# A two-layer audio tower: three normalizations moved from VectorE to ScalarE, a loop of four slots, fewer waits

## The reference, cut to what matters

```python
h = tok(x)                      # stride-2 convolution + mean of the pair, layernorm, gamma, beta -> (64, 188, 256)
h = h + attn0(layernorm(h))     # 16 heads of 16, softmax attention over the 64 sequences
h = h + ffn0(layernorm(h))      # gate, up (704) and down, inputs and weights rounded to blockwise fp4
h = h + attn1(layernorm(h))     # 16 heads of 64, causal linear attention over the 188 rows
h = h + ffn1(layernorm(h))      # layernorm again, dequantized fc1 (1024), silu, fc2, 0.5 * z

def _layernorm(x, axis=-1, eps=1e-05):
    m = jnp.mean(x, axis=axis, keepdims=True)
    ...
    return (x - m) / jnp.sqrt(v + eps)
```

## Time and profile before

| | us |
|---|---|
| median of 3 runs | 4795.0 (4787.19 to 4800.82) |
| the profiled execution | 4793.58 |
| its span on the core | 4791.8 |
| PE busy | 4454.1 (93%) |
| DVE busy | 3397.0 (71%) |
| ACT busy | 2495.3 (52%) |
| POOL busy | 1855.2 (39%) |

### The profile page before, as it was taken

One profiled execution on the slowest core, in us unless ns is written; L12 is line 12 of the kernel. 1 busy time (PEld: TensorE's weight loads), 2 busy tenths in 40 slices (PEclk: granted clock), 3 DMA queues, 4 the chain that ended last, 5 costly groups with the idle time before them and its releaser, 6 DMA issues.

```text
span 4791.8 us, 120275 instructions
## 1 busy us (share of the span) xinstructions
PE 4454.1 (93%) x43016; PEld 3973.3 (83%) x43016; DVE 3397.0 (71%) x7197; ACT 2495.3 (52%) x5314; POOL 1855.2 (39%) x2018
## 2 busy tenths in 40 slices
PE   3999999999999948999999999999999999999997
PEld 2888888888888847888888888888888888888886
DVE  5899999999999853666666666665666666666665
ACT  2555555555555524555554554554555555555553
POOL 1444444444444422343343343333334333334333
PEclk9999999999999979999999999999999999999998
DMA  2000000000000010000000000000000000000000
GB/s 82 19 23 23 23 23 23 23 23 23 23 23 23 22 41 8 5 15 8 8 11 11 8 8 15 8 8 15 8 8 11 11 8 8 14 8 8 15 5 11
DMA packets 64881, 78.93 MB, mean 16 GB/s; under 512 B 8759, under 2 KB 51127, under 8 KB 64439
## 3 DMA queue, kind: packets, MB, share of 16 engines
q1 hardware_dynamic: 64566, 74.07, 5.4%
HBM read 49.40 MB, written 24.64 MB: 15 GB/s over the span
## 4 chain that ended last, share of the span: by engine, by line
PE 45%; issue 9%; POOL 5%; DVE 2%; ACT 1%; POOLq 0%; DMA 0%; DVEq 0%; ACTq 0%; SPq 0%
PE bA L930 9%; PE bA L931 8%; PE bA L932 8%; PE bS L1216 3%; PE bO L1239 2%; PE bA L1303 2%; PE bB L930 2%; POOL sqs_lo L1636 2%; PE bB L1202 2%; PE bB L932 2%; PE bB L931 2%; PE bB L1203 2%; PE bA L1304 1%; PE bT L1256 1%; POOL yT_lo L1594 1%
## 5 line engine op out<-in xcount | busy, mean ns | idle before, releaser
L1636 POOL TENSOR_TENSOR sqs_lo<-sq,sqs_hi 128x768 fp32r<-128x768 f32 x256 | 471.4, 1842 | 811.7 <-ACT sqs_hi L1356 803.9
L1447 DVE TENSOR_TENSOR qk_lo<-bA,qk_hi 128x384 fp32r<-128x384 f32 x512 | 283.4, 553 | 626.4 <-ACT qk_hi L1356 626.2
L1375 ACT ACTIVATE phi<-bB 128x768 f32<-128x768 f32 x256 | 207.9, 812 | 681.2 <-PE bB L1203 681.2
L1594 POOL TENSOR_TENSOR yT_lo<-tanh_y,yT_hi 128x384 fp32r<-128x384 f32 x256 | 258.2, 1009 | 631.2 <-ACT yT_hi L1356 631.2
L1356 ACT ACTIVATE qk_hi<-bA 128x384 fp32r<-128x384 f32 x512 | 251.2, 491 | 229.6 <-PE bA L932 229.6
L1457 DVE TENSOR_TENSOR aT<-bS,mask 128x1024 f32<-128x1024 f32 x256 | 310.9, 1215 | 1.8 <-PE bS L1221 1.6
L930 PE MATMUL bA<-fc_lo,yT_hi 128*128 128x256 f32 x768 | 231.5, 301 | 60.9 <-POOL yT_lo L1594 34.2
L1365 ACT ACTIVATE sq<-bA 128x384 f32<-128x384 f32 x512 | 250.2, 489 | 61.7 <-DVE qk_lo L1447 61.6
L516 PE MATMUL bank<-down_sb,hqT 128*128 128x256 f32 x1128 | 278.5, 389 | 1.0 <-ACT hqT L598 1.0
L614 ACT ACTIVATE kblk<-gu,kb_masked,rowmask 128x128 f32<-128x128 f32 x752 | 270.7, 462 | 6.3 <-PE gu L540 6.3
L516 PEld LDWEIGHTS bank<-down_sb,hqT 128*128 128x128 f32 x1128 | 204.4, 190 | 52.6 <-issue 32.6
(11 more groups left out here) (243 smaller groups left out, 15025.4 us busy)
## 6 DMA issues: line engine op xcount, KB each, us to landing
xT<-in_x SPq DMA_DIRECT2D x94, 256.0 KB, 2.7
h_scratch<-h SPq DMA_DIRECT2D x188, 64.0 KB, 1.9
hx<-h_scratch SPq DMA_DIRECT2D x32, 256.0 KB, 2.7
out<-res SPq DMA_DIRECT2D x32, 256.0 KB, 2.1
hx<-h_scratch SPq DMA_DIRECT2D x64, 64.0 KB, 2.4
out<-res SPq DMA_DIRECT2D x64, 60.0 KB, 1.8
q<-in_fc_q SPq DMA_DIRECT2D x2, 1024.0 KB, 6.2
wq_sb<-in_wq SPq DMA_DIRECT2D x1, 1024.0 KB, 5.0
```

The source lines that it names most:

```text
L1447: dve.tensor_tensor(dst, src, hi.bitcast(fp32), ALU.subtract).then_inc(S[done], 1)
L1594: pool.tensor_tensor(yT[1][:, f % RING, :], tanh_y[f % 2][:], yT[0][:, f % RING, :].bitcast(fp32), ALU.subtract).then_inc(S["y_lo"], 1)
L1636: pool.tensor_tensor(sqs[1][:], sq[:], sqs[0][:].bitcast(fp32), ALU.subtract).then_inc(S["sq_lo"], 1)
```

## The change

Layer 0: `ln0_normalize` and `ln1_normalize` leave VectorE, and `xq_normalize` does too, as `ln2_normalize`. ScalarE now computes them as `Identity` activations with a row scale `rstd` and a row bias `nbias` = -mean x rstd, which POOL computes with two more one-column instructions in each `rsqrt`. VectorE's third `bn_aggr` moves ahead of its second gate step. Layer 1: the loop's body holds four slots instead of two (slots 3 to 26, six passes); `fc1` part 3 moves from step 4, place 1, to step 3, place 2, and `fc2` pair 0 the other way; waits that another wait implies are left out on TensorE.

```diff
@@ def normalize, ACT, layer 0 (the DVE functions of the same names are gone) @@
+                def normalize(dst, src, k, done):
+                    act.activation(dst, src, ACT.Identity, bias=nbias[:, k, :], scale=rstd[:, k, :]).then_inc(S[done], 1)
+
+                def ln0_normalize(t):
+                    wait(act, "rs0", t + 1, 4)
+                    wait(act, "gb_step", t, 3)
+                    wait(act, "ln1_ready", t)
+                    normalize(h0[:], y0[:], 0, "ln0")
...
+                def ln2_normalize(t, par):
+                    wait(act, "rs2", t - 1, 4)
+                    wait(act, "xq_step", t - 2, XQ)
+                    normalize(ln2[:], h1[par][:], 2, "ln2_ready")
@@ def slot, ACT, layer 0 @@
                     if exists(t, 2):
                         att_copy(t)
+                    if exists(t, 0):
+                        ln0_normalize(t)
                     if exists(t, 4):
                         hq_copy(t)
...
                     if exists(t, 3):
                         tanh(t - 3, 1)
+                    if exists(t, 0):
+                        ln1_normalize(t)
+                    if exists(t, 2):
+                        ln2_normalize(t, par)
+                    if exists(t, 3):
                         h1_copy(t, 1 - par)
@@ DVE, layer 0 @@
-                def normalize(dst, src, k):
-                    return dve.tensor_scalar(dst, src, moments[:, k, 0:1], rstd[:, k, :], ALU.subtract, ALU.mult)
...
                     if exists(t, 2):
                         row_statistics(h_st, 2, h1[par][:])
+                        row_moments(h_st, 2)
                     if exists(t, 3):
                         glu_gate(t - 3, 1)
                         glu_up(t - 3, 1)
-                    if exists(t, 0):
-                        ln1_normalize(t)
-                    if exists(t, 2):
-                        row_moments(h_st, 2)
-                    if exists(t, 3):
                         hq_scales(t - 3)
@@ def rsqrt, POOL, layer 0 @@
                     pool.tensor_tensor(rstd[:, k, :], moments[:, k, 1:2], eps[:, 0:1], ALU.add).then_inc(S[name], 1)
-                    pool.wait_ge(S[name], 2 * t + 1)
+                    pool.tensor_scalar(nbias[:, k, :], moments[:, k, 0:1], -1.0, None, ALU.mult).then_inc(S[name], 1)
+                    pool.wait_ge(S[name], 4 * t + 1)
                     pool.tensor_tensor(rstd[:, k, :], rstd[:, k, :], exponent[:, 0:1], ALU.pow).then_inc(S[name], 1)
+                    pool.wait_ge(S[name], 4 * t + 3)
+                    pool.tensor_tensor(nbias[:, k, :], nbias[:, k, :], rstd[:, k, :], ALU.mult).then_inc(S[name], 1)
@@ def slots, layer 1 @@
-            last = 3 + (SLOTS - 5) // 2 * 2
+            last = 3 + (SLOTS - 5) // UNROLL * UNROLL
...
-            with nc.Fori(3, last, 2, engines=(eng.engine,), hint_back_edge=True) as s:
-                slot(s, 1)
-                slot(s + 1, 0)
+            with nc.Fori(3, last, UNROLL, engines=(eng.engine,), hint_back_edge=True) as s:
+                for u in range(UNROLL):
+                    slot(s + u, (1 + u) % 2)
@@ def places, layer 1 @@
-            for f, (c, n) in enumerate(((2, 1), (2, 2), (3, 1), (4, 1), (4, 2), (5, 2), (6, 1), (7, 2))):
+            for f, (c, n) in enumerate(((2, 1), (2, 2), (3, 1), (3, 2), (4, 2), (5, 2), (6, 1), (7, 2))):
                 p[c][n] = ("fc1", s - 2, f)
-            p[3][2], p[5][1] = ("fc2", s - 2, 0, par), ("fc2", s - 2, 1, par)
+            p[4][1], p[5][1] = ("fc2", s - 2, 0, par), ("fc2", s - 2, 1, par)
@@ PE, layer 1: c1_qk; the same in c2_proj (qk_lo), c3_scores (phi_ready), c4_av (att1_step), @@
@@ c5_transpose (attT_hi), xn_transpose, h5_transpose, fc1 (hT_hi), fc2_pair (y_hi), wo_pair (attT_hi) @@
                     if c == 0:
-                        wait(pe, "xT_hi", s + 1, KC)
                         wait(pe, "xT_lo", s + 1, KC)
...
-                        read[i].extend((("qk_hi", 4 * g + (3 + i)), ("qk_lo", 2 * g + (1 + i))))
+                        read[i].append(("qk_hi", 4 * g + (3 + i)))
```

More of the change, by code:

```diff
@@ L54 @@
 RING = 4
+UNROLL = 4
 def wait_for(eng, sem, count, last, per=1):
@@ L677, in xq_copy, with ln1_normalize @@
                     copy(xqT[0][:], tp[:, 0:256].rearrange("p (c t) -> p c t", c=KC), "xqT_copied")
+                def normalize(dst, src, k, done):
[5 more added lines that the diff above has]
+                    normalize(h0[:], y0[:], 0, "ln0")
+                def ln1_normalize(t):
+                    wait(act, "rs1", t + 1, 4)
+                    wait(act, "ln1_transposed", t)
+                    normalize(ln1[:], h0[:], 1, "ln1_ready")
+                def ln2_normalize(t, par):
+                    wait(act, "rs2", t - 1, 4)
+                    wait(act, "xq_step", t - 2, XQ)
+                    normalize(ln2[:], h1[par][:], 2, "ln2_ready")
                 def slot(t, par):
@@ L733, in conv_read @@
                     wait(dve, "conv_done", t + 1)
+                    wait(dve, "ln0", t)
                     st = Steps(dve, S["y_step"], t, YS)
@@ L752, in score_shift @@
                     st.end()
[L754 to L757, removed]
                 def glu_gate(z, r):
@@ L786, in h1_add @@
                     return st
[L788 to L791, removed]
                 def h2_add(w, par):
@@ L797, in h2_add, with xq_scales @@
                     dve.tensor_tensor(h2[par][:], cv[:, 0:DM], h1b[par][:], ALU.add).then_inc(S["h2_ready"], 1)
-                def xq_normalize(y, par):
-                    wait(dve, "rs2", y + 1, 2)
+                def xq_scales(y):
+                    wait(dve, "xq_ready", y)
+                    wait(dve, "ln2_ready", y + 1)
                     st = Steps(dve, S["xq_step"], y, XQ)
-                    st.add(normalize(ln2[:], h1[par][:], 2))
+                    fp4_scales(dve, st, ln2[:], small_x, 128, DM)
                     return st
[L805 to L808, removed]
                 def xq_scaled(st):
@@ L1191, in c1_qk @@
                         last.then_inc(S["qk_done"], 1)
-                        read[i].extend((("qk_hi", 4 * g + (3 + i)), ("qk_lo", 2 * g + (1 + i))))
+                        read[i].append(("qk_hi", 4 * g + (3 + i)))
                 def c2_proj(g):
-                    wait_g(pe, "qk_lo", g + 1, 2)
                     wait_g(pe, "sq_lo", g + 1)
@@ L1206, in c3_scores @@
                 def c3_scores(g, b):
-                    wait_g(pe, "phi_ready", g + 1)
+                    if not has_chunk(g + 1):
+                        wait_g(pe, "phi_ready", g + 1)
                     wait_g(pe, "aT_ready", g)
@@ L1226, in c4_av @@
                     wait_g(pe, "aT_ready", g + 1)
-                    wait_g(pe, "att1_step", g, 3)
                     if c % 2 == 0:
@@ L1252, in c5_transpose @@
                     wait_g(pe, "att1_step", g + 1, 3)
-                    wait_g(pe, "attT_hi", g)
                     wait_g(pe, "attT_lo", g)
@@ L1286, in xn_transpose @@
                     for k in range(KC):
-                        read[k].extend((("xT_hi", s * 2 + (k + 1)), ("xT_lo", s * 2 + (k + 1))))
+                        read[k].append(("xT_lo", s * 2 + (k + 1)))
                 def h5_transpose(s):
@@ L1292, in h5_transpose @@
                     for k in range(KC):
-                        read[k].extend((("hT_hi", s * 2 + (k + 1)), ("hT_lo", s * 2 + (k + 1))))
+                        read[k].append(("hT_lo", s * 2 + (k + 1)))
                 def fc1(s, f):
                     if f == 0:
-                        wait(pe, "hT_hi", s + 1, KC)
                         wait(pe, "hT_lo", s + 1, KC)
@@ L1320, in fc2_pair @@
                 def fc2_pair(s, j, par):
-                    pe.wait_ge(S["y_hi"], s * FC + (2 * j + 2))
                     pe.wait_ge(S["y_lo"], s * FC + (2 * j + 2))
@@ L1325, in wo_pair @@
                 def wo_pair(s, j, par):
-                    pe.wait_ge(S["attT_hi"], s * CH + (2 * j + 2))
                     pe.wait_ge(S["attT_lo"], s * CH + (2 * j + 2))
```

10 lines of the change are left out of this document (4 added, 6 removed).

## The result

The changed kernel takes **4708.7 us** (median of 4 runs, 4704.83 to 4711.23) where the kernel before, run beside it, takes 4792.2 (4787.19 to 4800.82): a ratio of 0.9823, 95% interval 0.9806 to 0.984. The forecast was 4729 with a range of 4698 to 4770. The sign and the range held; the gain is 84 us where I forecast 66.

The account below looks back on a forecast made before the run. TensorE was taken to bound both layers, losing time in layer 1 at the loop end, `sq` waits and `fc2` stall. Terms -36 - 16 - 12 - 2 + 2 = -64 us gave 4729 us, range 4698 to 4770.

Parts of the forecast that it names:

- Loop end, 7 jumps x 5.1 = -36 us: Layer 1: a four-slot loop has seven jumps back fewer, each worth 5.1 us, saving 36 us.
- -2 us that I gave the swap for the clock: Layer 1: with the `fc2` stall shorter, some clock drops behind it may go, saving 2 us.
- Waits left out, -16 us: Layer 1: one needless wait less before V and `wo` products, 0.07 us each, eight a loop slot, saving 16 us.
- `fc1` 3 and `fc2` 0, -12 us (0.4 a slot): Layer 1: exchanging them leaves 1.4 of a 1.8 us stall, saving 0.4 us in each of 32 slots, 12 us.
- Case B: Layer 1: the `fc2` stall goes whole, another 44 us saved, total 4685 us; chance 6%.
- Layer 0, 0 a slot: Layer 0: moving three normalizations to ScalarE changes no slot, since TensorE sets the pace and ScalarE's new work fits.
- +2 for the first slots: Layer 0's first slots, where nothing overlaps: 0.5 us longer for each of four normalizations in the chain, costing 2 us.
- case C: Layer 0: VectorE sets the pace, so its 1.2 us relief saves 113 us over 94 slots, about 4616 us; chance 5%.
- A: Layer 1: jumps cost by body length, 10.2 instead of 5.1 us, giving back 26 us, total 4755 us; chance 10%.
- charge on VectorE: Layer 1 loop: by the skill's 512-instruction fetch window, VectorE's branch begins to pay in the longer pass; no firm size.
- D: Layer 0: ScalarE late if POOL's new instructions cost 0.55 us, +108 us, about 4837; chance 5% in full, 8% mild.

Follow-up runs that it names:

- e4_layer0: Kernel before with only layer 0's change, its three normalizations moved to ScalarE: 4793.6 us, ratio 0.9994.
- e6_head87: Kernel before, all waits kept, with the layer 1 loop's first TensorE instruction set at place 87 of its 256-instruction block: 4752.1 us, ratio 0.9921.
- e10_head167: Kernel before, all waits kept, with the layer 1 loop's first TensorE instruction set at place 167 of its 256-instruction block: 4749.1 us, ratio 0.9915.
- e12_after_two_head87: Changed kernel with two slots per jump instead of four and the loop's first TensorE instruction set at place 87 of its block: 4720.5 us, ratio 0.9853.
- e2_waits: Kernel before with only the implied waits left out on TensorE in layer 1, loop of two slots: 4728.5 us, ratio 0.986.
- e7_waits_head167: Kernel before with the implied waits left out and the loop's first TensorE instruction set at place 167 of its block: 4721.4 us, ratio 0.9859.
- e9_after_two: Changed kernel with two slots per jump instead of four, all else as changed: 4710.5 us, ratio 0.9833.
- e3_swap: Kernel before with only `fc1` part 3 and `fc2` pair 0 changing places: 4772.5 us, ratio 0.995.
- e1_unroll: Kernel before with only layer 1's loop changed, to four slots per pass: 4751.2 us, ratio 0.9905.
- e13_act_twice: Changed kernel with each of layer 0's three normalizations made twice by ScalarE, once into an unread tensor: 4731.6 us, ratio 0.9878.
- e11_after_head87: Changed kernel with its loop's first TensorE instruction set at place 87 of its block: 4705.0 us, ratio 0.982.

## Why the prediction was right, and where it was not

*Loop end, 7 jumps x 5.1 = -36 us.* **This step failed in its price.** The count, seven jumps fewer, is right. But I held the price fixed and changed only the number. The jumps cost 12 x 5.35 = 64.2 us before and 5 x 1.80 = 9.0 after: -55. The price before has three parts: the first stop, a median 2.2 us; the second stop, 0.9 to 1.6 behind two jumps of three, which I had not seen; and the clock, which in the loop was at 0.50 for 51 us before and for 3.4 after. If half of that time is lost, it is an estimated 26 / 12 = 2.1 us a jump; the three shares are rough, for e4_layer0 pays about the same for its jumps (63.3 us) with longer first stops and 37.5 us at the low clock. Three of its eleven stretches, 3.4 us each, stand not at the jump but 49 us behind it, at the `fc2` stall:

```profile
2267.30:2270.70 3.40, 3.40 (x16) 3.40 (x17) 1.59 (x4) 0.41 (x1) 0.00 (x0) 0.50 0.00 0
```

At this stall stand also all the low stretches of e6_head87 (five) and e10_head167 (three), whose jumps are cheap; the runs with `fc1` 3 and `fc2` 0 exchanged have none there. So the -2 us that I gave the swap for the clock was a real term, and more like -5 (three stretches of 3.4 us, half lost: an estimate).

In the changed kernel only the first stop is left:

```profile
2741.39 0.34 PE L1308 MATMUL bA<-hT_hi,fc_w 128*128 128x384 f32 x1
2743.27 0.43 PE L938 MATMUL bB<-qk_lo,omega_hi 128*128 128x384 f32 x1 [1.54 <-issue]
...
2745.10 0.34 PE L938 MATMUL bA<-xT_lo,wq_hi 128*128 128x384 f32 x1
```

And the number of jumps, which I credited, is not what the gain hangs on: with two slots to a pass the same kernel takes 4710.5 us, its twelve jumps 10.6 us. It hangs on where the loop's code lies, and the other parts of the change moved that; the number counts only where jumps are dear, as in e12_after_two_head87.

*Waits left out, -16 us.* Right as a term, wrong as an account of the edit. The mechanism is as forecast. The load behind `sq` in the loop, after, against the earlier trace rows:

```profile
3570.11 0.48 ACT L1367 ACTIVATE sq<-bA 128x384 f32<-128x384 f32 x1
3570.65 0.19 PEld L938 LDWEIGHTS bA<-wv_lo,xT_hi 128*128 128x128 f32 x1 [0.17 <-ACT sq L1367]
```

Over some 200 of these places in the loop the median from the end of `sq` to the load is 0.051 us, before 0.122: 0.071 saved, and 0.07 forecast. Eight in a slot are 0.57, and slots went from 89.39 to 88.78 in e2_waits. Alone the edit brought 68 us, because taking instructions out moved the loop: its jumps cost 13.7 us in all, and so do those of e10_head167, which has every wait and another place.

*`fc1` 3 and `fc2` 0, -12 us (0.4 a slot), and -2 for the clock.* The mechanism is right, the size a little off. The step after the change, against the earlier trace rows:

```profile
3586.00 0.65 ACT L1407 ACTIVATE pre<-bA,fc1b,fc1s 128x384 f32<-128x384 f32 x1
...
3586.70 0.44 PE L1307 MATMUL bA<-hT_lo,fc_w 128*128 128x384 f32 x1 [1.17 <-ACT pre L1407]
3586.75 0.62 DVE L1517 SCALAR_TENSOR_TENSOR pre<-bA,fc1s,pre 128x384 f32<-128x384 f32 x1 [0.75 <-ACT pre L1407]
...
3586.98 0.34 PE L1308 MATMUL bA<-hT_hi,fc_w 128*128 128x384 f32 x1
...
3587.42 0.19 PEld L1307 LDWEIGHTS bA<-hT_lo,fc_w 128*128 128x128 f32 x1 [0.42 <-DVE pre L1517]
```

The first half waits 1.17 us for ScalarE, less than the old 1.75. The second half waits again, for VectorE, which has the second bank until 3587.37: its first product starts with the load at 3587.42, 0.44 us behind the product before it, where a free one follows in 0.17, so 0.27 is lost a second time. 1.75 - 1.17 - 0.27 = 0.31 us a slot; the slots show 0.25 (88.76 in e7_waits_head167, 88.51 in e9_after_two), and 0.16 in e3_swap. Over 32 slots that is 5 to 8 us and not 12. Case B, the stall gone whole, needed the bank free earlier, and it was not.

*Layer 0, 0 a slot, +2 for the first slots.* The zero is right, for the reason given, and with it case C is refuted: VectorE was relieved and the slot stayed. (I had taken all three normalizations at the 0.40 us of the earlier trace rows, which is `h0`'s alone; the other two took VectorE 0.361 us each, so 1.13 us left it a slot and not 1.2.) The +2 has the wrong sign. The first `y` is read 0.9 us sooner and the next four intervals are 63.1 us together where they were 65.9; the last `y` comes at 1670.5 instead of 1676.1. The run with layer 0's change alone shows the same (63.1 us, 1671.0). I had counted the longer chain of ScalarE and POOL. What I had not counted, as I read it, is that in the slots where TensorE does not set the pace VectorE does, and that it had shed work. No run shows that reading by itself.

*The rivals.* A, jumps that cost by the length of the body: refuted. A body of 7742 instructions in e1_unroll pays 1.7 us where 3884 pay 2.2, and at good places 7589 and 3884 both pay 0.36. VectorE's branch went from 0.061 to 0.068 us, with 857 recorded instructions of its stream in a pass instead of 438. So the rule of the Trainium skill ("Runtime: NRT & Kernel Launch", Instruction fetch mechanics) that I had let speak for a charge on VectorE is not borne out here. These loops hint their jump back (`hint_back_edge=True`, a `BRANCH_PREFETCH_HINT` row of each engine in every pass), and that may be why; no run was made without the hint. D: POOL's new instructions came out at 0.22 and 0.19. e13_act_twice shows how near ScalarE is: with three more activations a slot it begins to cost.

*The sum* in the terms of the prediction, in us: jumps and clock -55 (-38 forecast), up to the first `xn` -6, nearly all of it layer 0's (+2 forecast), and the rest of layer 1, for waits and swap, what is left of its -77 and -3: -24 (-28 forecast). Together -85, the difference of the two spans.

## What to carry to other kernels

The price of a loop's jump back on a busy TensorE is not, in these runs, a property of the loop's size. Before unrolling, move the loop's head within its block and see what the jump costs, and look too at what comes right behind the loop, where e11_after_head87 lost most of what it had gained; and when an edit that only adds or drops a few instructions changes the time by a per cent, look at the branch before crediting the edit. When parts of a change cut the same cost, try each on top of the others: alone, these four promised 140 us and gave 84 together. A needless wait between a producer's end and the consumer that it holds up was worth 0.07 us here, in the median of some 200 places.

## What the hardware showed that I had not expected

One and the same loop of TensorE, with no other instruction changed, took 4790 or 4749 us by where its code lies (ratio 0.9915, 0.99 to 0.993). The branch itself ran from 0.35 to 3.5 us. Behind a dear jump a second stop of 0.9 to 1.6 us came 24 instructions into the loop. And a stop can cost more than itself: in the kernel before, eleven stretches of the loop ran at the 1.2 GHz level, eight at the jumps and three at the `fc2` stall of 1.75 us; with stops of 1.4 to 1.9 us, no second one and the stall cut to 1.17, as in the changed kernel, one did; in e9_after_two, with stops of 0.35 to 1.6 us, none.

And layer 0 has a wait that no semaphore shows. VectorE's first `small_x` operation, 128x16, whose like takes 0.17 us; before:

```profile
808.61 1.40 POOL L112 TENSOR_TENSOR hh<-hh,small 128x704 f32<-128x704 f32 x1 [0.86 <-DVE small L106]
...
809.25 0.78 DVE L102 TENSOR_SCALAR small_x<-small_x 128x16 f32<-128x16 f32 x1
810.07 0.17 DVE L104 TENSOR_SCALAR small_x<-small_x 128x16 f32<-128x16 f32 x1
```

and after:

```profile
804.87 1.39 POOL L113 TENSOR_TENSOR hh<-hh,small 128x704 f32<-128x704 f32 x1 [1.23 <-DVE small L107]
805.10 1.19 DVE L103 TENSOR_SCALAR small_x<-small_x 128x16 f32<-128x16 f32 x1
806.32 0.17 DVE L105 TENSOR_SCALAR small_x<-small_x 128x16 f32<-128x16 f32 x1
```

In both it ends 0.02 to 0.04 us behind POOL's product, in each of the 76 slots between 200 and 1500 us, however early it begins (809.25 + 0.78 and 808.61 + 1.40; 805.10 + 1.19 and 804.87 + 1.39). So VectorE, which lost the normalization that stood ahead of it, arrives sooner and is held longer: 0.40 us of each slot's relief came back as a longer `small_x` (its mean went from 0.785 to 1.184 us). Case C had counted on the whole relief. The Trainium skill ("GPSIMD Engine Reference", section Specifications) has the two engines share their interfaces to SBUF, and contend where VectorE runs in a two-port mode or with two inputs there; the trace shows the holding, not its cause.
